# A pre-norm attention and look-up FFN block: the norm of the Gram tiles moved from ScalarE to VectorE, look-up steps placed anew

## What is computed

```python
def attn(x, Wq, Wk, Wv, Wo):
    q, k, v = x @ Wq, x @ Wk, x @ Wv
    scores = einsum('bes,bfs->bef', qT, kT) / sqrt(16)      # 512 x 512 per batch, over the sequence
    weights = softmax(scores, axis=-1)
    return swapaxes(einsum('bef,bfs->bes', weights, vT), 1, 2) @ Wo

def ffn(x, lut, gate_idx, up_idx, down_idx):               # every weight is lut[idx], 16 entries
    h = silu(x @ lut[gate_idx].T) * (x @ lut[up_idx].T)     # 512 -> 1376
    return h @ lut[down_idx].T                              # 1376 -> 512

x = x + attn(layernorm(x), Wq, Wk, Wv, Wo)
x = x + ffn(layernorm(x), lut, gate_idx, up_idx, down_idx)
```

## Time and profile before

| what | value |
|---|---|
| median of 3 runs | 1051.66 us (1051.18 to 1052.39) |
| the profiled execution | 1051.26 us, its span 1049.5 us |
| PE busy | 1006.6 us, 96% of the span |
| DVE, ACT, POOL busy | 489.5, 465.4, 137.6 us (47, 44, 13%) |
| granted TensorE clock, mean | 0.997 |

### The profile page before, as it was taken

The page is one execution under the profiler, slowest core; times in us unless marked ns, Lnnn a source line. Parts: engine busy times, 40 slices in busy tenths (PEclk is TensorE's granted clock), DMA queues, the critical chain, the costliest instruction groups (busy, mean ns, idle before and its releaser), DMA issues.

```text
span 1049.5 us, 13011 instructions
## 1 busy us (share of the span) xinstructions
PE 1006.6 (96%) x4744; PEld 830.7 (79%) x4744; DVE 489.5 (47%) x1016; ACT 465.4 (44%) x753; POOL 137.6 (13%) x135
## 2 busy tenths in 40 slices
PE   4979999999999899999999999999999999999997
PEld 4867877788788668888888888888888888888885
DVE  5798999989999942311131113111311131212101
ACT  5999999797989821221222122212221222122110
POOL 4521000000000000110111011101110111011110
PEclk9999999999999999999999999999999999999999
DMA  8962012121111182200220002002200020000000
GB/s 275 296 220 94 18 56 88 34 101 46 51 49 69 65 299 81 101 1 1 81 81 1 1 1 81 1 1 81 81 1 1 1 81 1 1 1 41 1 1 40
DMA packets 31756, 66.04 MB, mean 63 GB/s; under 512 B 3584, under 2 KB 17168, under 8 KB 27088
## 3 DMA queue, kind: packets, MB, share of 16 engines
q1 hardware_dynamic: 26912, 63.06, 16.8%
q10 hardware_dynamic: 4752, 2.16, 0.7%
q0 software_dynamic: 32, 0.01, 0.1%
HBM read 44.18 MB, written 21.04 MB: 62 GB/s over the span
## 4 chain that ended last, share of the span: by engine, by line
PE 85%; DVE 6%; ACT 4%; issue 3%; POOL 1%; DMA 0%; POOLq 0%; ACTq 0%; DVEq 0%
PE bank L1015 45%; PE bank L1023 22%; PE bank L957 13%; PE bank L1058 3%; PE bank L971 1%; PE bank L1004 1%; DVE part L1202 1%; DVE bn L1179 1%; DVE picked L1202 1%; ACT part L748 0%; DVE smax L1366 0%; ACT xg_n L851 0%; DMA xg<-in_L_attn_x 0%; ACT idx_out L841 0%; ACT xn_first L804 0%
## 5 line engine op out<-in xcount | busy, mean ns | idle before, releaser
L1015 PE MATMUL bank<-x2t_hi,w_hi 128*128 128x512 f32 (+1 forms) x704 | 275.3, 391 | 7.2 <-DVE w_lo L1218 3.9
L1015 PE MATMUL bank<-x2t_hi,w_lo 128*128 128x512 f32 (+1 forms) x704 | 274.8, 390 | 0.0
L1015 PE MATMUL bank<-x2t_lo,w_hi 128*128 128x512 f32 (+1 forms) x704 | 274.8, 390 | 0.0
L1417 DVE TENSOR_TENSOR h_full<-bank,h_gate 128x512 f32<-128x512 f32 (+1 forms) x66 | 45.6, 691 | 396.7 <-PE bank L1015 396.7
L1015 PEld LDWEIGHTS bank<-x2t_hi,w_hi 128*128 128x128 f32 (+1 forms) x704 | 130.7, 186 | 37.9 <-DVE w_lo L1218 4.8
L748 ACT ACTIVATE part<-high_bit,lut,lut_step 128x512 f32<-128x512 uint8 x198 | 153.8, 813 | 14.4 <-DVE part L1202 10.2
L1015 PEld LDWEIGHTS bank<-x2t_lo,w_hi 128*128 128x128 f32 (+1 forms) x704 | 130.8, 186 | 29.6
L1015 PEld LDWEIGHTS bank<-x2t_hi,w_lo 128*128 128x128 f32 (+1 forms) x704 | 130.7, 186 | 29.4
L930 ACT ACTIVATE h_gate<-bank 128x512 f32<-128x512 f32 (+1 forms) x66 | 39.4, 598 | 256.5 <-PE bank L1015 256.5
L697 POOL TENSOR_TENSOR h_lo<-h_full,h_hi 128x512 fp32r<-128x512 f32 (+1 forms) x66 | 85.2, 1290 | 508.3 <-ACT h_hi L933 508.3
L1023 PE MATMUL bank<-w_hi,h_hi 128*128 128x512 f32 (+1 forms) x324 | 129.6, 400 | 0.1
(11 more groups left out here) (148 smaller groups left out, 1329.8 us busy)
## 6 DMA issues: line engine op xcount, KB each, us to landing
xg<-in_L_attn_x SPq DMA_DIRECT2D x8, 1024.0 KB, 6.5
out_dram<-x1a SPq DMA_DIRECT2D x5, 1024.0 KB, 3.9
x1a<-in_L_attn_x SPq DMA_DIRECT2D x4, 1024.0 KB, 4.8
x1b<-in_L_attn_x SPq DMA_DIRECT2D x3, 1024.0 KB, 4.9
m_hi<-m_scratch SPq DMA_DIRECT2D x3, 1024.0 KB, 4.8
m_lo<-m_scratch SPq DMA_DIRECT2D x3, 1024.0 KB, 6.9
out_dram<-x1b SPq DMA_DIRECT2D x3, 1024.0 KB, 3.9
idx_raw<-in_L_ffn_gate_idx SPq DMA_DIRECT2D x10, 256.0 KB, 6.3
```

Of the source, the lines that this page charges most:

```text
L1015: last = pe.matmul(tile[0:n, :], a, x, start=(k == 0 and j == 0), stop=(k == K - 1 and j == 2))
L1417: dve.tensor_tensor(h_full[0:n, :], bank[5][0:n, :], h_gate[0:n, :], ALU.mult).then_inc(h_done, 1)
```

## The change

`gram_n` leaves ACT's walk through the list and enters DVE's, at the same entries. The ACT activation (Identity, with a per-partition scale and bias) becomes one `tensor_scalar` of DVE with the same two per-partition scalars (mult, add). Its two waits go with it: for the group's `xg_stats`, which is DVE's own `stats_shift`, and for `xg_lo_done` of tile i - 4, also DVE's own. Operands, buffers, semaphores and all other stages stay, and ACT's cast still waits for `xg_normed`. The second part is the two strings: the same steps in the same order, at other entries.

```diff
--- before.py
+++ after.py
@@ -423,20 +423,20 @@
         timeline.append(("y", 1))
 
         ACT_LOOKS = (
-            "0000000000000000000000000000000000000000000000000000000000000000000000000000000000000001000000000000"
-            "1000000000101000000000000000000000030000000000000000000000000000000004000300000000000000000000000000"
-            "0000000300000000000000000000000000000000300000000000000000300000000010020200000000000500301020040030"
-            "0400300300500020000020000040000020000200002000040002000000000000000000000000000000600030000300400300"
-            "0030030000200500002002000200005000000010103000000003040000300000600205000020000007000100030500000000"
-            "020000060400060400304001050005050010500204000504003040020500040600106001080003050020400103"
+            "0000000000000000000000000000000000000000000000000000000000000000000000000000000000000000000000000000"
+            "0000000040000000010000000000000000000000000000000000000000000000000002000000000002000000000000000000"
+            "0000000000000000000000000000000000000000000000000000000000000000000010020400000000000300401030030040"
+            "0300400200400030000030000020000020000400002000020003000000000000000000000000000000400030000400300400"
+            "0020040000300300001005000100003002000000105000000002050000200000800005000030000008000100030500000000"
+            "02000005060006040020400104000605002040020d0006040020500107000405001050020c0005040020400001"
         )
         DVE_LOOKS = (
-            "0000000000000000000000000000000000000000000000000000000000000000000000000000000000000000020000000001"
-            "0000000000000000000000010000000300000000000000000400000000000000000005000000030000000000000000000000"
-            "0000200000000000000200000000000000000010000000000003000000300000030000100000070000000070030005006004"
-            "0040050040026000030000040000060000030000300006000040300000000000000000000000000000070003000040060030"
-            "00045000000430000006200000420003000070011000600000003010200100900000a0200000008030006010007010000000"
-            "00200000d02000d020070200702000d010060100803000c010080200604000d020050400902000c050040300b"
+            "0000000000000000000000000000000000000000000000000000000000000000000000000000000000000000000000000200"
+            "0000000000000000000000000000000000000000000000000000000000000000000007000000000000000000000000000000"
+            "00000000000000000000000000000000000000000000000000000000001000000000000000000e0000000040060004004006"
+            "0030040060024000060000040000030000060000400003000050200000000000000000000000000000030004000060030040"
+            "00063010000350100002300000530002000090001000600000003040100100700000a0200000009030007000007020000000"
+            "00400000d02000c020070300501000d010080300k02000c020060400702000c040050300j02000c020060400401"
         )
 
         def with_looks(counts, steps):
@@ -841,15 +841,6 @@
                     act.copy(dst, src).then_inc(idx_laid, 1)
                     if 4 <= u < 7:
                         fetch_idx(u - 4)
-                if stage == "gram_n":
-                    i = arg
-                    g, t = i // T, i % T
-                    act.wait_ge(xg_stats, g + 1)
-                    if i >= 4:
-                        act.wait_ge(xg_lo_done, i - 3)
-                    scale, bias = scale_of(g)
-                    act.activation(xg_n[i % 4][:], xg[g % 3][:, t, :], ACT.Identity, bias=bias[:, t:t + 1],
-                                   scale=scale[:, t:t + 1]).then_inc(xg_normed, 1)
                 if stage == "gram_in":
                     i = arg
                     act.wait_ge(xg_normed, i + 1)
@@ -1342,6 +1333,15 @@
                     stats_var(g + 1)
                 if stage == "stats_shift":
                     stats_shift(arg + 1, *scale_of(arg), xg_stats)
+                if stage == "gram_n":
+                    i = arg
+                    g, t = i // T, i % T
+                    dve.wait_ge(xg_stats, g + 1)
+                    if i >= 4:
+                        dve.wait_ge(xg_lo_done, i - 3)
+                    scale, bias = scale_of(g)
+                    dve.tensor_scalar(xg_n[i % 4][:], xg[g % 3][:, t, :], scale[:, t:t + 1], bias[:, t:t + 1],
+                                      ALU.mult, ALU.add).then_inc(xg_normed, 1)
                 if stage == "gram_low":
                     i = arg
                     dve.wait_ge(xg_hi_done, i + 1)
```

## The result

Median 1060.03 us (6 runs, 1058.25 to 1062.51) against 1052.17 for the kernel before beside it (6 runs, 1051.18 to 1054.45): the ratio is 1.0070, with a 95% interval of 1.0054 to 1.0086. So the change costs 7.9 us. I had forecast 1056.5, a range of 1047 to 1062, and "slower" as the likeliest sign. The profiled execution of the kernel after lasts 1060.16 us, its span 1058.4; the span before was 1049.5.

A forecast was written before the change was run, and what follows sets the result against it. PE was taken to set the end, with DVE nearly as full ahead of 371.2 us. Gram stage -2.4 and last ten pairs +7.2 gave +4.8 us on 1051.26: 1056.1, or 1056.5 for the median, range 1047 to 1062.

The forecast's parts named there:

- The sign: Whole kernel: slower, chance 0.58, against 0.22 for faster and 0.20 for within 0.2% of no change.
- the likeliest case: Whole kernel: the forecast of 1056.5 us itself, chance 0.52, with norms of 0.40 to 0.52 us on DVE.
- The price of a norm: On DVE: one norm takes 0.45 us from start to start, with 0.27 and 0.60 kept as bounds.
- The collisions: Gram stage: DVE instructions run longer beside POOL's index casts, between 0 and 4.4 us for 31 norms, taken as 1.9.
- the cheap-norm rival: On DVE: a norm costs 0.27 us, 5.6 us less for 31, giving 1050.9 us, no change; chance 0.20.
- The dear one: Rival on DVE: a norm costs 0.60 us like a plain subtraction and collides at full price, 1063.7 us; chance 0.08.
- The Gram stage: Up to 99.5 us: ends 2.4 us sooner, 0.9 up to 50 us and 1.5 after it.
- they fit in the idle time: Up to 50 us: about 15 norms, 6.8 us, go into DVE's 8.7 us of idle time; taken as -0.9 us.
- The middle: Products and pairs up to (1,3): same work in the slots, and a lead of 2.4 us is carried through.
- The last ten pairs: After (1,3): 15 more look-up steps on DVE cost 7.2 us, as PE waiting for `w_lo` at (0,7) and (0,9).
- DVE has no room: After pair (1,3): DVE has 66.94 us of work in 68.7, so 7.2 us more come out as PE waits.
- Relief of ACT: Rival, whole kernel: DVE waits for ACT, and an emptier ACT ends all 15.7 us of it; 1047.3 us, chance 0.20.

The follow-up runs named there:

- the twelve early norms: Kernel before with its own strings, norm of tiles 0 to 11 on DVE and of tiles 12 to 31 on ACT: 1053.94 us, ratio 1.0021.
- norm only: Kernel after with both look-up strings of the kernel before, so all norms on DVE: 1060.24 us, ratio 1.0079.
- the three other kernels with the new strings: New strings with the norm on ACT (1060.9 us), with the norm left out (1056.87), and the kernel after with DVE's own leaves of tiles 2 to 32 made by POOL (1059.77).
- the leaves on POOL: Kernel before with DVE's own leaf of tiles 2 to 32 made by POOL: 1051.29 us, ratio 1.0005; measured again with four leaves a few entries earlier: 1050.72, 0.9986.

## Why the prediction was right, and where it wasn't

**The sign** was right, and the time is within the range of 1047 to 1062: 3.5 us above the forecast and outside the likeliest case's own 1053 to 1060 by a hair. The size was not: the sum -2.4 + 7.2 = 4.8 met +8.7 in the profiled executions, nearly twice as much. That the range held is in part luck, since the mechanisms of both terms come out differently.

**The price of a norm** by itself was right: 0.44 to 0.45 us from start to start, 0.53 to 0.55 long. So were the busy times built on it: +4.8 forecast and +5.3 measured up to 50 us, +1.7 and +2.0 from there to 99.5. The collisions were set too low. The means are 0.629 and 0.644 us, not "near 0.54", which is some 3 us over 32 norms where 1.9 were taken; and the low parts got longer too, from 700 to 767 ns in the mean, 2.1 us that the sum didn't have. The prediction also counts 31 norms where the kernel has 32, three of them before 13 us by its own reading; that is worth less than 1 us. The figure of the Trainium skill (VectorE: DVE Perf Modes, the section on the TRN2 errata), 0.33 us, is not what this instruction takes with two per-partition scalars. The same section of the Trainium skill adds that this row is too low and that the fixed term measured there is about 150 cycles; by that the estimate would be 406 cycles or 0.42 us, near the 0.44 from start to start and still below the 0.53 that the instruction lasts. The measurement decides, and the cheap-norm rival falls. The dear one is nearer than it looks, with 0.55 us in the mean against its 0.60, but its 1063.7 us were not reached.

**The Gram stage** was the step that failed: -2.4 forecast, +0.35 measured. Two terms of it. First, "they fit in the idle time": with the old strings the twelve early norms cost 2.4 us at the end of the stage in spite of 8.7 us of idle time, and all 32 cost 12.4 of some 14. The idle time in front of `xg_lo` was part of the chain from tile to tile (this is argued from that run; no run takes the chain apart), and only the postponed look-up steps (8.8 us between norm only and the kernel after) paid for the norms. PE's idle time did fall, by 1.8 us. Second, PE was 2.1 us slower on the same matmuls, a term that the prediction didn't have.

**The middle** was to carry the lead through. It lost 1.9 us: 0.2 of idle time and 1.7 of slower PE, most of it the stretch at 149 us behind the 2.23 us wait for `mat_x_lo`.

**The last ten pairs** were near in size, 7.2 forecast and 6.5 measured, and right in place, (0,7) and (0,9), with 2.15 us more at (0,8). The size is in part luck. The waits are 4.4 us longer and not 7.2 (8.3 in all, not the 11 that the prediction named); the other 2.1 are PE's slower matmuls, and 1.5 of them come from where a slow stretch happened to fall, for the three other kernels with the new strings lose only some 5 us here. And "DVE has no room" is not what sets the wait at (0,7): with 14 us less in DVE's queue it is 3.33 us, and the time is the same with either strings. Three kernels with the new strings in which the norm is on ACT, on DVE or nowhere have 3.39, 3.38 and 3.37 us there. What the traces show is an order: the `w_lo` that PE needs stands ten steps behind an `h_full` that PE itself has just released, and PE has one gate product of work meanwhile. The prediction had counted the steps, 11 to 22, in that very slot, and priced them as load over the whole stretch. That moving those steps alone would remove the wait is argued from the traces; no run did it.

**The rivals.** Relief of ACT was false where it counts: ACT's load in the Gram stage fell by 27.7 us and DVE's 6.1 us of waits for `xg_hi` went to nil, but with no norm at all on either engine the stage ends only 3.2 us sooner with the old strings (the median is 5.3 lower) and 7.0 with the new ones (4.0 lower). Relief can't give more than that. With the norm on DVE the stage is 9.2 us later with the old strings and 1.8 sooner with the new ones, which the last ten pairs and PE's slow stretches take back.

No kernel here beats the one before beyond doubt: with the leaves on POOL it is at 1.0005 and 0.9986.

## What to carry to other kernels

An edit that hands work to a full engine and re-plans the queue around it is two edits: run each alone, and the work left out too, before the sum is believed. Here each alone cost 8 to 9 us and both together 8, in different stages. Where a queue is placed by hand, look for the slot, not the load: count what stands between an instruction that the bounding engine releases and the one that it needs next. Idle time of an engine inside a producer chain need not be room.

## What I had not expected

Idle time of PE of 2 to 3 us was often followed by seven or more matmuls at half speed, some 1.5 us for seven, which makes such a wait dearer than it looks, unless the next wait is for the same late engine and takes it in. POOL beside DVE gives little: its instructions last 2 to 3 times DVE's (1.52 against 0.69 us for a low part, 1.45 against 0.54 for a leaf), and DVE's leaf beside them doubles, 0.54 to 1.04, while predicated copies stay at 0.74.
